# Gates of a mixture of experts: from sixteen spreading products to a DMA through DRAM, with the schedule around it rewritten

## The chip, the cores and the metric

The kernel runs on one core of one Trainium2 chip. The metric is the device time of one execution in microseconds. An engine is named as in the profile: PE is TensorE, DVE is VectorE, ACT is ScalarE, POOL is GpSimd, SP is SyncE.

## What is computed

One block over an input of 16 images of 56 x 56 tokens with 32 channels: windowed attention (windows of 7 x 7, shifted by 3, four heads of 8 channels, a bias table and a mask added after the softmax), a residual, and a mixture of experts with a residual. Cut to what matters:

```python
x = x + conv(layernorm(x))            # windowed attention, then out @ w_proj + b_proj
t = to_tokens(x)
probs = softmax(ln(t) @ router_w + router_b)      # 8 experts
top_p, top_i = top_k(probs, 2); top_p /= sum(top_p)
expert_out = einsum('bnd,edc->bnec', ln(t), expert_w) + expert_b
t = t + einsum('bnk,bnkc->bnc', top_p, take(expert_out, top_i))
```

## The kernel before

The work is cut into 16 units of 3136 tokens: two images, half of the columns. A tile of tokens has 112 partitions (image and row) with 28 tokens of 32 channels (896 elements). For products the channels of four tokens stand on 128 partitions (A = 4), with 784 columns.

The stages of a unit, with their names in the code and the lines of the profile:

- load (SP, L505, twelve DMAs into xin) and keep (SP, L512, one DMA xin to x_kept, two buffers; it waits until the residual of the unit two earlier, `back` 1, has read that buffer). The load of the next unit waits until keep has landed.
- norm1: a sum on DVE (L844), centring on POOL (L556), squares on ACT (L681), their sum on DVE (L850), then on POOL a scaling, an epsilon and a power of -1/2 (L567), and a multiplication (L571). norm2 is the same on the residual (L856, L579, L690, L862, L590, L594).
- xt (PE transposes L1111, ACT), qk (four products of 128x128 weights, L1119), place (POOL, q masked by head, L603) and kmask (ACT, k masked by head, L721), v (L1128), ob (L1143).
- attention in four groups. Of each: products for the maximum (PE L1161 into ps_win), the maximum and its split in two bf16 parts (DVE L866, L880, L882), their turn (PE L1169), a copy mr (ACT L766), the scores with the maximum taken off (PE L1184, L1190, into ps_win again), exponentials (ACT L776), products with v (PE L1205), a reciprocal and a product (DVE L889, L893) and the bias part added (POOL L611).
- ot (turned output), y (projection L1228, with b_proj added by a product of three bf16 parts, L1225), back (the residual on DVE, L907).
- x2t, router (PE L1251, tokens stationary), top2 (22 small steps on DVE and POOL: the two largest of eight logits, their shares, then the shares split in three bf16 parts), wt (turned to 96 x 784), mix (sixteen products L1273, each spreading one row group of shares over 128 partitions in ps_weight, each followed by a DVE product with the tokens, L979), the expert products (PE L1287 into ps_acc), final.
- replicate (SP, L522 and L525): the normalized tokens are copied so that each expert's 32 partitions hold them (x4). store (SP, L531).

Every engine runs the same generated list, `program`, and takes its own steps out of it, strictly in order. `macro_step` yields the four groups of one unit and, between their steps, the side tasks of `SIDE_TASKS`: of the unit after (xt, qk, v, ...), of the one after that (load, norm1), of the one before (y, norm2, router, top2) and of the one before that (mix, final, store). A place (g, p) of the table stands behind the scores (0), the maximum (1), the pv (2) and the shift (3) of group g. PE transposes and products of the side tasks share one PSUM bank, ps_shared, the mix has ps_weight, the expert sums ps_acc, the attention ps_win (four banks) and ps_pv.

## Time and profile before

| what | time |
|---|---|
| median of 3 runs | 838.19 us |
| lowest and highest | 836.32, 843.77 us |
| the profiled execution | 836.74 us |
| its span, first to last instruction | 834.9 us |
| mean granted clock of TensorE | 0.908 of full |
| busy: PE, DVE, ACT, POOL | 676.2, 547.7, 386.1, 486.1 us |

The span is what the rows below add up to; 1.8 us of the execution lie around it. In these rows a line with x16 is a group of sixteen instructions, the number before the engine is the start, the next the duration, and a bracket at the end is the idle time of that engine before it, with what ended it.

### The profile page before, as it was taken

The page shows a single profiled execution, that of the slowest core. Times are in us where ns is not written, and L with a number is a line of the kernel's source. Part 1 is how long each engine was busy: PE and PEld are TensorE (multiplying, and loading weights), DVE is VectorE, ACT ScalarE, POOL GpSimd, SP SyncE. Part 2 cuts the span into 40 slices and gives each one's busy share as a digit, 9 for nine tenths or more (in the row PEclk, how much of TensorE's full clock was granted, in tenths as well). Part 3 has the DMA queues.
Part 4 walks back from the last instruction along what each step waited for, and adds up shares of the span by engine and source line. Part 5 has one row for each costly group of instructions (what it writes and reads, how often), then busy time and mean ns, then how long its engine had stood idle before and what let it go on. Part 6 is the DMA issues. An engine that isn't in the chain of part 4 may idle for free.

```text
span 834.9 us, 29295 instructions
## 1 busy us (share of the span) xinstructions
PE 676.2 (81%) x12514; PEld 443.7 (53%) x12514; DVE 547.7 (66%) x999; ACT 386.1 (46%) x705; POOL 486.1 (58%) x539
## 2 busy tenths in 40 slices
PE   0787879888887879889797988888898988878666
PEld 0465555655556556546565554555656655645331
DVE  6242657768586767678676667857676767766443
ACT  1645464646364455626464463635355563622110
POOL 4616676575757666664757566574766666541520
PEclk9979989999999999988989889999999999997555
DMA  4100221413231131413231131323223230403040
GB/s 128 30 3 3 57 62 41 90 50 79 61 79 50 32 79 47 93 41 79 60 80 50 28 84 41 79 59 69 51 50 70 54 86 22 88 13 79 20 97 19
DMA packets 19008, 48.11 MB, mean 58 GB/s; under 512 B 9536, under 2 KB 9536, under 8 KB 17344
## 3 DMA queue, kind: packets, MB, share of 16 engines
q1 hardware_dynamic: 18448, 45.06, 23.3%
q8 instruction: 99, 1.62, 0.8%
q10 hardware_dynamic: 432, 1.19, 0.4%
q14 instruction: 29, 0.24, 0.1%
HBM read 7.69 MB, written 6.42 MB: 17 GB/s over the span
## 4 chain that ended last, share of the span: by engine, by line
PE 45%; DVE 32%; issue 11%; ACT 6%; POOL 4%; DMA 0%; SPq 0%; DVEq 0%; ACTq 0%; POOLq 0%
DVE mx L866 9%; PE ps_shared L1119 6%; PE ps_win L1190 6%; PE ps_acc L1287 5%; PE ps_pv L1205 5%; PE ps_shared L1143 4%; PE ps_weight L1273 4%; PE ps_win L1161 4%; PE ps_shared L1228 3%; DVE zt L979 3%; DVE x L979 3%; DVE x L907 2%; PE ps_win L1184 2%; DVE ms L880 2%; ACT ot L754 2%
## 5 line engine op out<-in xcount | busy, mean ns | idle before, releaser
L866 DVE TENSOR_REDUCE mx<-ps_win 128x32 f32<-128x1568 f32 x64 | 114.5, 1789 | 64.6 <-PE ps_win L1161 64.1
L979 DVE TENSOR_TENSOR zt<-ps_weight,x 128x392 f32<-128x392 f32 x118 | 66.1, 561 | 89.5 <-PE ps_weight L1273 89.0
L776 ACT ACTIVATE pt<-ps_win 128x784 f32<-128x784 f32 x128 | 98.4, 821 | 44.0 <-PE ps_win L1190 43.6
L1273 PE MATMUL ps_weight<-wt,const_bf_tile 96*128 96x392 bf16 x234 | 84.1, 359 | 41.1 <-DVE zt L979 20.7
L611 POOL TENSOR_TENSOR on<-on,obs 128x256 f32<-128x256 f32 x64 | 46.6, 729 | 120.0 <-DVE on L893 92.6
L1205 PEld LDWEIGHTS ps_pv<-vb,pt 128*49 128x49 f32 x4096 | 104.9, 129 | 15.3 <-issue 13.0
L1205 PE MATMUL ps_pv<-vb,pt 128*49 128x18 f32 x4096 | 109.7, 201 | 0.0
L979 DVE TENSOR_TENSOR x<-ps_weight,x 128x392 f32<-128x392 f32 x116 | 65.4, 564 | 38.3 <-PE ps_weight L1273 36.9
L766 ACT COPY mr<-ps_win 128x512 bf16<-128x512 bf16 x64 | 37.5, 587 | 95.8 <-PE ps_win L1169 95.8
L1190 PE MATMUL ps_win<-qbd,kp 32*49 32x196 f32 x2048 | 79.0, 370 | 0.0
L590 POOL TENSOR_TENSOR st<-st,minus_half 112x28 f32<-112x28 f32 x16 | 77.0, 4812 | 1.3
L567 POOL TENSOR_TENSOR st<-st,minus_half 112x28 f32<-112x28 f32 x16 | 76.9, 4809 | 1.3
L603 POOL TENSOR_SCALAR qbd<-qp,const_tile 128x392 f32<-128x392 f32 x128 | 76.6, 611 | 0.2 <-issue 0.2
L1273 PEld LDWEIGHTS ps_weight<-wt,const_bf_tile 96*128 96x128 bf16 x234 | 23.5, 100 | 87.7 <-DVE zt L979 41.4
L721 ACT ACTIVATE kbd<-kp,const_tile 128x392 f32<-128x392 f32 x128 | 69.3, 620 | 0.0
L1119 PE MATMUL ps_shared<-xt,folded_tile 128*128 128x392 f32 x124 | 66.3, 621 | 1.8 <-ACT xt L699 0.7
L1161 PE MATMUL ps_win<-kbd,qp 32*49 32x196 f32 x2048 | 59.0, 338 | 7.4 <-ACT pt L776 6.8
L699 ACT ACTIVATE xt<-ps_shared 128x448 f32<-128x448 f32 (+1 forms) x31 | 16.4, 528 | 85.5 <-PE ps_shared L1111 85.5
L1161 PEld LDWEIGHTS ps_win<-kbd,qp 32*49 32x49 f32 x2048 | 35.0, 120 | 34.1 <-ACT pt L776 25.0
L744 ACT COPY obs<-ps_shared 128x256 f32<-128x256 f32 x62 | 20.1, 375 | 55.8 <-PE ps_shared L1143 55.8
L1190 PEld LDWEIGHTS ps_win<-qbd,kp 32*49 32x49 f32 x2048 | 42.1, 131 | 4.2
L1169 PE MATMUL ps_win<-const_bf_tile,ms 128*128 128x128 bf16 x256 | 27.1, 232 | 20.4 <-DVE ms L882 20.1
(134 smaller groups left out, 1318.8 us busy)
## 6 DMA issues: line engine op xcount, KB each, us to landing
x<-x SPq DMA_DIRECT2D x48, 392.0 KB, 5.1
x_kept<-xin SPq DMA_DIRECT2D x16, 392.0 KB, 3.4
x<-x2t SPq DMA_DIRECT2D x64, 98.0 KB, 2.2
xin<-x SPq DMA_DIRECT2D x32, 150.0 KB
out<-xo SPq DMA_DIRECT2D x32, 150.0 KB
xin<-x SPq DMA_DIRECT2D x32, 18.0 KB
out<-xo SPq DMA_DIRECT2D x32, 18.0 KB
weight_tile<-weights ACTq DMA_DIRECT2D x1, 560.0 KB, 4.6
```

The costliest lines, as they stand in the source:

```text
L567: nc.gpsimd.tensor_tensor(st1[:, 4, :], st1[:, 3, :], minus_half[:, :], ALU.pow).then_inc(rstd1, 1)
L590: nc.gpsimd.tensor_tensor(st2[:, 4, :], st2[:, 3, :], minus_half[:, :], ALU.pow).then_inc(rstd2, 1)
L603: nc.gpsimd.tensor_scalar(qbd[i][:, :, h, :], qp[v.par][:, 8 * i:8 * i + 8, :], head_rows[:, h:h + 1], 1.0, ALU.mult, ALU.mult).then_inc(q ...
L721: ins = nc.scalar.activation(kbd[i][:, :, h, :], kp[v.par][:, 8 * i:8 * i + 8, :], ACT.Copy, scale=head_rows[:, h:h + 1])
L776: nc.scalar.activation(pt[g % 2][:, k, :, :, :].rearrange("p a h n -> p a (h n)"), ps_win[:, :, HN * k:HN * k + HN], ACT.Exp).then_inc(pro ...
L866: nc.vector.tensor_reduce(mx[g % 2].rearrange("n a x h -> n a (x h)"), ps_win[:, :, 0:8 * N].rearrange("n a (k m) -> n a k m", m=N), AX, A ...
L979: nc.vector.tensor_tensor(tokens if eh else zt[:, a, :], weight_bank(w, 1 + i)[:, 0:HALF], tokens, ALU.mult).then_inc(weight_drained, 1)
L1119: mm(pre_bank(v, 2 + i)[:, 0:HALF], (wk if i % 2 else wq)[:, :], xt[:, 8 * b:8 * b + 8, :, :].rearrange("p q k i -> p (q k i)"), start=Tru ...
L1161: ins = mm(ps_win[PAD * k:PAD * k + N, a, HN * x:HN * x + HN], qp[u.par][r, q, :], kbd[g // 2][r, q % 8, :, :].rearrange("p h n -> p (h n) ...
L1190: ins = mm(ps_win[PAD * k:PAD * k + N, a, HN * x:HN * x + HN], kp[u.par][r, q, :], qbd[g // 2][r, q % 8, :, :].rearrange("p h n -> p (h n) ...
L1205: ins = mm(ps_pv[PAD * x:PAD * x + N, c0:c0 + SLOT], pt[g % 2][:, x, a, h, :], vb[u.par][:, 2 * g + x, a, h, :], start=True, stop=True)
L1273: mm(weight_bank(w, 1 + i)[:, 0:HALF], weight_sel[:, eh, a, :], wt[:, HALF * half:HALF * half + HALF], start=True, stop=True).then_inc(wei ...
```

## The change

Eight edits, of which the first brings most of the new code.

1. The sixteen products that spread the shares are gone, and with them the three bf16 parts, wt and ps_weight. The shares (98 partitions, f32) are turned on PE, drained by ACT, written by SP to a DRAM tensor (four DMAs), and read back with a source stride of zero over the 32 partitions of an expert (eight DMAs into `gates`, four for experts 0 to 3, four for 4 to 7). The multiplication with the tokens is split between DVE and POOL (`mul`, half each), and the expert sums (`sum`) run over a left part of 448 and a right part of 336 columns.
2. ps_weight becomes a second bank of ps_shared; all side fills alternate between the two, and a fill waits for the drain two fills back.
3. The router keeps its weights stationary (`route`) and its result is turned (`logits`): the top 2 work on 98 partitions with 32 tokens.
4. q and k are each made by products on 64x64 quadrants (`project`), both halves together.
5. The root is found without a power: ACT takes a logarithm and an exponential (`norm_scale`), DVE makes one Newton step in three instructions (`norm_root`), POOL multiplies. The table of ACT is loaded once, ahead of everything, in both kernels.
6. b_proj is added by POOL to the kept input (`kept`), not by a product.
7. The second half of kmask goes from ACT to POOL.
8. The table of side tasks, the prologue and the tail are written anew.

The core of the diff:

```diff
 SIDE_TASKS = {
-    (0, 0): [("ot", 1), ("keep", 0), ("wt", 0), ("y", 0), ("mix", 0), ("back", 0), ("mix", 1), ("y", 1), ("back", 1), ("norm2_center", 0)],
...
-    (1, 0): [("qk", 0), ("load", 0), ("mix", 5)],
...
-    (2, 0): [("mix", 8), ("x2t", 0), ("norm1_center", 0), ("mix", 9)],
...
+    (0, 1): [("load", 0), ("y", 0)],
+    (0, 2): [("back", 0), ("share", 0), ("q", 0), ("y", 1)],
+    (0, 3): [("back", 1), ("gates", 0), ("norm2_center", 0)],
+    (1, 0): [("k", 0), ("norm1_center", 0)],
...
+            def gate_rows(w, _):
+
+                sp.wait_ge(shares_drained, upto("shares_drained", w))
...
+                for b in range(4):
+                    sp.dma_start(shares_kept[:, BLOCK * b:BLOCK * b + BLOCK],
+                                 shares[32 * b:32 * b + 32, :]).then_inc(shares_stored, 16)
+                sp.wait_ge(shares_stored, upto("shares_stored", w))
...
+                for eh in range(2):
+                    for e in range(4):
+                        rows = bass.AP(shares_kept.tensor, shares_kept.offset + (4 * eh + e) * COLS,
+                                       [[0, C], [E * COLS, A], [1, COLS]])
+                        sp.dma_start(gates[C * e:C * e + C, eh, :, :], rows).then_inc(gates_high if eh else gates_low, 16)
...
-                nc.gpsimd.tensor_tensor(st1[:, 4, :], st1[:, 3, :], minus_half[:, :], ALU.pow).then_inc(rstd1, 1)
...
+                nc.scalar.activation(st1[:, 1, :], st1[:, 2, :], ACT.Ln, bias=eps1[:, 0:1]).then_inc(log1, 1)
...
+                nc.scalar.activation(st1[:, 3, :], st1[:, 1, :], ACT.Exp, scale=-0.5, bias=guess_scale[:, 0:1]).then_inc(guess1, 1)
...
+            def mul(w, i):
+
+                eh, half = divmod(i, 2)
+                dve.wait_ge(x4_ready, upto("x4_ready", w))
+                if eh:
+                    dve.wait_ge(gates_high, upto("gates_high", w))
+                else:
+                    dve.wait_ge(gates_low, upto("gates_low", w))
+                gate = gates[:, eh, 0:2, columns(half)]
+                nc.vector.tensor_tensor(gate, gate, x4[w.par][:, 0:2, columns(half)], ALU.mult).then_inc(gated, 1)
...
+                for b in range(2):
+                    for r in range(2):
+                        rows, to = slice(64 * r, 64 * r + 64), 64 * (r ^ b)
+                        ins = mm(halves[b][to:to + 64, 0:HALF], w64[rows, rows],
+                                 xt[rows, 8 * b:8 * b + 8, :, :].rearrange("p q k i -> p (q k i)"), start=True, stop=True)
```

Three places of the new order. First VectorE, from the residual (back 0 and 1, writing x) over the sum of norm2 to the loaded input's sum (st<-xin), in one unit. Before:

```order
L907 TENSOR_TENSOR x_1<-ps_shared,x_kept 112x3x4x32
L856 TENSOR_REDUCE st<-x_1 112x28
L866 TENSOR_REDUCE mx<-ps_win 128x32
...
L866 TENSOR_REDUCE mx<-ps_win 128x32
...
L979 TENSOR_TENSOR zt<-ps_weight,x_0 128x392
L844 TENSOR_REDUCE st<-xin 112x28
L979 TENSOR_TENSOR zt<-ps_weight,x_0 128x392
L866 TENSOR_REDUCE mx<-ps_win 128x32
```

and in the changed kernel, where gates<-gates is the multiplication of a half of the low gates:

```order
L999 TENSOR_TENSOR x_0<-ps_shared,x_kept 112x3x4x32
L934 TENSOR_REDUCE st<-x_0 112x28
L908 TENSOR_REDUCE st<-xin 112x28
L958 TENSOR_REDUCE mx<-ps_win 128x32
L972 TENSOR_SCALAR ms<-mx 128x8x4
L974 SCALAR_TENSOR_TENSOR ms<-mx,ms 128x8x4
L981 RECIPROCAL rz<-ps_pv 128x32
L985 TENSOR_TENSOR on<-ps_pv,rz 128x16x2x8
L940 TENSOR_REDUCE st<-sq 112x28
...
L1061 TENSOR_TENSOR gates<-gates,x_1 128x2x448
L958 TENSOR_REDUCE mx<-ps_win 128x32
```

The input's sum has moved from behind two maxima after the residual to right behind the sum of norm2, and a wait for gates stands ahead of the third maximum.

Second SyncE's queue, from keep to the copies of the tokens. Before:

```order
L512 DMA x_kept<-xin 112x896
L505 DMA xin<-x 48x800
...
L505 DMA xin<-x 3x96
L522 DMA x_1<-x2t 32x784 x4
L525 DMA x_1<-x_1 32x3136 x3
```

and in the changed kernel:

```order
L495 DMA x_kept<-xin 112x896
L488 DMA xin<-x 48x800
...
L488 DMA xin<-x 3x96
L519 DMA shares_kept<-shares 32x196 x4
L528 DMA gates<-shares_kept 32x4x784 x8
L506 DMA x_0<-x2t 32x784 x4
```

The twelve transfers that were in the queue between keep and the copies are still there, and four writes and eight reads of the gates have come in behind them.

Third ScalarE, around the copy mr of group 2. Before:

```order
L776 ACTIVATE pt<-ps_win 128x784 x2
L710 ACTIVATE qp<-ps_shared 128x392
L714 COPY kp<-ps_shared 128x392
L766 COPY mr<-ps_win 128x512
L710 ACTIVATE qp<-ps_shared 128x392
```

and in the changed kernel, where st<-st,eps is the logarithm and st<-st,guess_scale the exponential:

```order
L803 ACTIVATE pt<-ps_win 128x784 x2
L740 COPY kp<-ps_shared 128x392 x2
L704 ACTIVATE sq<-xc 112x896
L760 COPY vb<-ps_shared 49x64x8 x2
L818 ACTIVATE st<-st,eps 112x28
L822 ACTIVATE st<-st,guess_scale 112x28
L793 COPY mr<-ps_win 128x512
```

The logarithm and the exponential, which take VectorE's sum of squares, stand ahead of mr.

## Rows read from the trace of the kernel before

**Rows 1.** Windows: length, busy PE, PEld, DVE, ACT, POOL, clock, DMA share, GB/s

```profile
0.00:39.30 39.30, 17.01 (x157) 10.11 (x157) 19.77 (x46) 14.34 (x26) 21.56 (x32) 0.96 0.29 84
...
120.60:685.50 564.90, 483.10 (x9386) 321.16 (x9385) 403.33 (x720) 287.65 (x529) 363.92 (x397) 0.95 0.27 62
...
640.80:685.50 44.70, 38.10 (x772) 25.66 (x770) 33.05 (x60) 23.89 (x45) 30.26 (x33) 1.00 0.28 65
...
775.40:834.90 59.50, 37.48 (x161) 16.04 (x161) 27.05 (x56) 5.73 (x10) 13.27 (x13) 0.53 0.21 46
```

**Rows 2.** Timeline of one group of the unit, all engines

```profile
656.36 1.79 DVE L866 TENSOR_REDUCE mx<-ps_win 128x32 f32<-128x1568 f32 x1 [1.14 <-PE ps_win L1161]
...
658.19 0.24 DVE L880 TENSOR_SCALAR ms<-mx 128x32 bf16<-128x32 f32 x1
...
659.07 0.35 DVE L889 RECIPROCAL rz<-ps_pv 128x32 f32<-128x32 f32 x1
...
659.25 0.59 ACT L766 COPY mr<-ps_win 128x512 bf16<-128x512 bf16 x1 [1.61 <-PE ps_win L1169]
...
659.45 0.42 DVE L893 TENSOR_TENSOR on<-ps_pv,rz 128x256 f32<-128x256 f32 x1
...
660.66 0.67 PE L1190 MATMUL ps_win<-qbd,kp 32*49 32x196 f32 x16
```

**Rows 3.** Lines of PE within that unit (busy us, mean ns | idle before)

```profile
L1205 PE MATMUL ps_pv<-vb,pt 128*49 128x18 f32 x256 | 6.6, 198 | 0.0
...
L1273 PE MATMUL ps_weight<-wt,const_bf_tile 96*128 96x392 bf16 x16 | 5.4, 337 | 3.2 <-DVE x L979 1.7 <-DVE zt L979 1.4
...
L1119 PE MATMUL ps_shared<-xt,folded_tile 128*128 128x392 f32 x8 | 3.6, 532 | 0.1
...
L1228 PE MATMUL ps_shared<-weight_tile,ot 128*112 128x128 f32 x14 | 1.9, 273 | 0.0
...
L1111 PE MATMUL ps_shared<-const_tile,xc 112*128 112x112 f32 x7 | 1.0, 263 | 0.5 <-POOL xc L571 0.5
```

**Rows 4.** Lines of DVE and POOL within that unit

```profile
L979 DVE TENSOR_TENSOR zt<-ps_weight,x 128x392 f32<-128x392 f32 x8 | 4.5, 560 | 5.9 <-PE ps_weight L1273 5.9
...
L567 POOL TENSOR_TENSOR st<-st,minus_half 112x28 f32<-112x28 f32 x1 | 4.8, 4807 | 0.1
```

**Rows 5.** Timeline of PE, from the last maximum to the next scores

```profile
676.17 0.91 PE L1161 MATMUL ps_win<-kbd,qp 32*49 32x196 f32 x32
...
684.41 0.67 PE L1190 MATMUL ps_win<-qbd,kp 32*49 32x196 f32 x16
```

**Rows 6.** Timeline of SP's queue in the prologue and that unit, and of DVE

```profile
13.62 4.27 SPq L505 DMA_DIRECT2D xin<-x  x12
...
19.04 0.53 SPq L512 DMA_DIRECT2D x_kept<-xin  x1
...
646.82 1.09 DVE L856 TENSOR_REDUCE st<-x 112x28 f32<-112x896 f32 x1
...
647.17 0.54 SPq L512 DMA_DIRECT2D x_kept<-xin  x1
...
650.59 4.28 SPq L505 DMA_DIRECT2D xin<-x  x12
...
665.19 2.44 SPq L522 DMA_DIRECT2D x<-x2t  x4
...
669.23 2.43 SPq L525 DMA_DIRECT2D x<-x  x3
```

**Rows 7.** Windows while constants are loaded and while x2t is copied

```profile
4.00:5.00 1.00, 0.00 (x0) 0.00 (x0) 0.89 (x3) 0.00 (x0) 0.00 (x0) 1.00 0.99 381
...
667.00:668.00 1.00, 0.91 (x10) 0.80 (x9) 0.99 (x3) 0.59 (x2) 0.53 (x1) 1.00 0.82 185
```

**Rows 8.** Timeline of POOL and DVE, one pass beside a small instruction

```profile
648.31 1.75 POOL L579 TENSOR_TENSOR xc<-x,st 112x896 f32<-112x896 f32 x1
...
649.64 0.51 DVE L880 TENSOR_SCALAR ms<-mx 128x32 bf16<-128x32 f32 x1
```

More of the change, by code:

```diff
@@ L20 @@
+import math
 from contextlib import ExitStack
@@ L166, in macro_step, with program @@
         yield from side((g, 3))
-def program(eng):
-    unit = [fixed(n) for n in range(UNITS)] + [None, None]
+def program():
+    unit = [None, None] + [Unit(n) for n in range(UNITS)] + [None, None]
     seen = []
@@ L543, in _ @@
                     replicate(unit, i)
+                elif step == "gates":
+                    gate_rows(unit, i)
                 elif step == "store":
@@ L805, in _ @@
             act.dma_start(const_bf16_tile[:, :], consts_bf16).then_inc(weights_loaded, 16)
-            for step, unit, i in program(act):
+            for step, unit, i in program():
                 if step == "norm1_square":
@@ L1043, in _ @@
             ones(vb[0])
-            for step, unit, i in program(dve):
+            for step, unit, i in program():
                 if step == "norm1_center":
@@ L1048, in _ @@
                     norm1_scale(unit, i)
+                elif step == "norm1_root":
+                    norm1_root(unit, i)
                 elif step == "norm2_center":
@@ L1298, in _ @@
             mm(ps_acc[:, 0:FOLDED], part["centre"], part["raw"], start=True, stop=True).then_inc(centred_weights, 1)
-            for step, unit, i in program(pe):
+            for step, unit, i in program():
                 if step == "xt":
```

669 lines of the change are left out of this document (353 added, 316 removed), and 16 rows, old and new, of tables (PROLOGUE, SIDE_TASKS, TAIL, per_unit).

## The prediction, made before the changed kernel was run

> **What bounds the kernel now.** I read the windows by stretch first, then the busy time by line within one undisturbed unit, then the timeline of that unit, and last the DMA queue of SyncE. The kernel is one loop over 16 units, and no stretch of it looks unlike the rest: from the scores of unit 2 to those of unit 14, twelve units take 564.9 us, 47.1 us each, with TensorE at 0.95 of its full clock; the undisturbed unit from 640.8 takes 44.7 us and keeps TensorE busy for 38.1 of them, VectorE for 33.1, GpSimd for 30.3, ScalarE for 23.9 [rows 1]. So TensorE is nearest to being the bound, but not alone: a unit holds four groups, and each group is a serial chain through one PSUM tile, ps_win. From the start of the maximum on VectorE to the start of ScalarE's copy mr it takes 2.9 us (maximum 1.8, two small instructions, and 0.5 for the turn on TensorE), the copy 0.6, and the scores end 1.5 us after it, of which I count 1.4 [rows 2]. Ahead of it come the exponentials and the products for the maximum. Whatever is queued ahead of one of these steps on its engine and waits, delays the unit.
>
> **What leaves TensorE.** The 16 products that spread the weights over partitions are 5.4 us of TensorE per unit and another 3.2 of waiting for VectorE [rows 3]. The projections, 3.6 us per unit, are cut into 64x64 quadrants; that they run side by side is what the products on 32-row tiles already do, so I take half, 1.8 us. Together TensorE falls by about 7 us per unit, from 38 to 31. VectorE loses 16 products of 0.56 us, 9.0 in all, and gets four multiplications of 896 or 672 elements, about 1.1 and 0.8 us by the 1.09 us of its reduction over 896 [rows 4, 6]. GpSimd loses two powers of 4.8 us and gets half of the k masks, the bias on the kept input and four multiplications of up to 1.7 us, which is what a pass over 896 elements takes it [rows 4, 8]. Every engine gets room. If nothing new waited, I work a unit out at 43 us below.
>
> **What is moved, and what is queued behind it.** Here the order decides. All times are from the end of a unit's first scores (time 0); the walk follows the program's order with the durations of the rows.
>
> Step 1, until back 1. The roots, three small VectorE instructions (0.2 each as an estimate, about half the 0.35 of the reciprocal in [rows 2]), and GpSimd's 1.7 [rows 8] now stand ahead of xt: 2.3. Then on TensorE xt 1.0, maximum 0.9, y 0 1.0, pv 1.6; on VectorE the reciprocal and product of pv 0.8 and back 0 0.6 (like a product of 392 elements); q 0.9, its drain 0.5 (mr's copy of 512 columns takes 0.59), y 1 0.9, back 1 0.6 [rows 2 to 5]. Sum: 11.1, say 11.
>
> Step 2, the load. keep copies xin into a buffer that back 1 of the unit two earlier reads last, so on SyncE it waits for back 1, as before; but the load now stands right behind it and the sum over the loaded input (norm1_center) stands two VectorE instructions after back 1, ahead of the next maximum. Before, the sum came more than a group later. From the rows: back 1 ends where the sum behind it starts, at 646.8, keep is issued at 647.17, the load may start at 650.59, so 3.8 us; and from the load's first issue at 13.62 to the instruction that waited for its landing 5.4 us [rows 6]. The input is there at 11 + 3.8 + 5.4 = 20.2. VectorE has 1.1 us of work in between (the sum of norm2), so it stands for about 8 us, and the maximum of group 2, whose products TensorE has ready at about 15, starts at 20.2 + 1.1 = 21.3 in place of 15. I find no cover: TensorE can do pv and v meanwhile and is then idle.
>
> Step 3, the second scores. The small instructions of the maximum end at 23.7. ScalarE's logarithm and exponential of norm2 now stand ahead of its copy mr and wait for VectorE's reciprocal and product (0.8) and the reduction over squares (1.1); with 0.5 for the two themselves (an estimate by VectorE's small ones of 0.24 and 0.35), mr starts at 26.1, ends at 26.7, and the scores end at 28.1. The same happens one group later with norm1. Each costs 2 us where the power on GpSimd had cost this path nothing.
>
> Step 4, the gates. SyncE ends the issue of the load at 11 + 3.8 + 4.3 = 19.1. Four small writes of the shares follow, and the reads wait for them: four copies out of x2t, equally many, let the next transfer start 4.0 us after the first issue [rows 6], so the reads start at 23.1. They are eight of 401 KB (32 partitions, 4 runs of 3136 bytes), 3.2 MB per unit. The trace of before has no such read. The nearest rows are the x2t copies, with the same run and the same 32 partitions: 185 GB/s at a share of 0.82, 226 GB/s full; the upper end is the load of the constants, 381 GB/s at 0.99 [rows 7]. I take 226, the nearer: 7.1 us for the low half and 14.2 for both, after 2.3 us of fixed time (4.0 less 0.4 MB at 226). Low lands at 32.5, high at 39.6. At 381 they land at 29.6 and 33.8. A source row that 32 partitions read at once could also be slower, for which no row gives a price; I bound it at half the rate, 39.6 and 53.8.
>
> Step 5, the third and fourth scores. VectorE's first multiplication waits for low ahead of the third maximum: 32.5 + 1.1 = 33.6, the maximum's small instructions end at 36.0, norm1's reduction, logarithm and exponential as in step 3 give 38.4, mr and scores 40.4. The third multiplication on GpSimd is done at 39.6 + 1.7 = 41.3; sum 1 on TensorE waits for it, ahead of the next unit's maximum: 42.2 (0.9, as one projection has it, since its four products use different columns of the array), maximum 43.1. From the end of this maximum to the end of the scores the unit before took 8.0 us (677.08 to 685.08, [rows 5]); one more sum of 0.9 stands in it now. The unit ends at 52.0.
>
> **The Trainium skill against this.** A small VectorE instruction took 0.51 us at 649.64 while GpSimd ran its 1.75 us pass, and 0.24 in the quiet group [rows 2, 8]. "SBUF — State Buffer", section "SBUF: two separate sides", says that a VectorE instruction with two SBUF inputs and a GpSimd instruction that reads SBUF exclude each other for the whole instruction. The multiplications on both engines are released by the same transfer, so by that rule the third maximum could come 1.7 us later than I have it; the trace agrees in kind. Likewise "DMA: Bandwidth & Descriptors", section "Latency and other measured facts", says that the receipt is the fixed part of a transfer and slowest from HBM, so the writes of the shares may cost more than my 4.0 us; no row here shows it.
>
> **The sum.** Up to the first scores of unit 0: 39.3 [rows 1], less one power of 4.8 for about 1.3 of its successor, and some of the bias preparation: 34.8. The next two units took 81.3 (39.3 to 120.6); the first has no stall (SyncE is ahead), the second has the load but no gates: 38 + 46 = 84. Twelve units of 52: 624. The last two took 89.9; without loads, with gates on a free queue, 85. The tail took 59.5 [rows 1]: the last unit's roots save 4, but the way from the shares to the products is a write and 3.2 MB of reads (20 us) where 16 products took some 14 us, net 61. Sum: 34.8 + 84 + 624 + 85 + 61 = 889, against a span of 834.9; with the 1.8 us that lie around the span (836.7 executed, within the 836.3 to 843.8 of the runs, whose median is 838.2) 891.
>
> **Rivals.** (a) Faster: the waits don't bind. Mechanism: if the load lands within 4 us of back 1, and the gates before the third maximum, the unit is the walk without them: scores at 21.9, maximum at 24.3, 31.1, and 43 at the end; all in all 776 us. It decides at 47.5 us a unit, above which the kernel is slower. For it: TensorE gives up 7 us, and VectorE waits 5.9 us in a unit for those products alone. Against it: 3.8 and 5.4 us are in the trace and the order leaves no room. (b) Reads at 381 GB/s: the third maximum is then held only by step 3, the unit takes 49.6, the kernel 862. (c) The clock and the port: TensorE idles 5 us twice per unit. In the tail, with gaps of that kind, its clock was 0.53 [rows 1]. At 1.2 GHz turn and scores cost 1.7 us more twice, and shared reads as much: 55.5 a unit, 933. (d) The reads from one row are slow, half the rate: 66 a unit, with the tail and the last two units 1090. (e) All within 1%: a unit of 47 to 48, part of each wait.
>
> **How the numbers follow.** My forecast holds 0.50, (a) 0.14, (b) 0.13, (c) 0.13, (d) 0.06, (e) 0.04. The time is that of the forecast, 891, whose own range is 870 to 915. The range of 830 to 950 leaves out (a) and (d). Runs of this kernel spread by about 1%, which is what can be told. Faster: (a), 0.14; within 1%: 0.04; slower: the rest, 0.82.
>
> **What would show it.** In the profile of the changed kernel the VectorE reduction over xin (L908) should be idle for about 7 to 8 us before each of 13 units, put down to the DMA into xin; the first multiplication (L1061) should wait 4 to 6 us on the DMA into gates; mr (L793) should wait longer in groups 2 and 3 than in 1; TensorE should be busy for about 31 us of a 52 us unit with a clock below 0.9. A loaded input within 5 us of back 1, or gates that land before the third maximum's products, would make the prediction wrong on the fast side; gates reads far under 226 GB/s on the slow side.

## The result and the profile after

| what | time |
|---|---|
| changed kernel, median of 4 runs | 1011.36 us (1011.17 to 1012.46) |
| before, median of 4 runs | 837.26 us (834.82 to 843.77) |
| ratio | 1.207, 95% interval 1.200 to 1.214 |
| span of the profiled execution | 1009.6 us, TensorE's granted clock 0.757 |

Ratios and their intervals, here and below, leave out executions more than 1.5% slower than the fastest of the same kernel; medians do not.

Slower, as forecast, but by 174 us where 53 were forecast, and outside the range. The windows of the changed kernel, with the columns of [rows 1]: one unit from back 1 to back 1, twelve units, all behind them, and inside the unit the stretch from the turn of group 2's maximum to that of group 3's.

```profile
437.60:496.10 58.50, 41.39 (x751) 26.68 (x751) 36.09 (x54) 23.83 (x47) 32.52 (x32) 0.76 0.48 107
143.90:846.80 702.90, 488.77 (x9156) 319.74 (x9140) 424.31 (x637) 282.38 (x552) 389.42 (x384) 0.77 0.48 107
846.80:1009.60 162.80, 84.68 (x1345) 50.28 (x1345) 79.91 (x120) 37.32 (x74) 71.16 (x56) 0.66 0.58 125
449.00:466.00 17.00, 11.04 (x171) 6.84 (x175) 12.94 (x17) 7.32 (x15) 13.61 (x11) 0.54 0.93 198
```

A unit takes 58.6 us (702.9 / 12) where it took 47.1, and no engine is busy for more than 42 of them: the kernel waits. TensorE is busy for 41.4 us of the unit, where I had forecast about 31. Between 449 and 466 the clock is 0.54, so nearly at its lower level of 1.2 GHz, after TensorE had stood for 5 us.

The groups by line over the whole execution, which answer to [rows 3, 4]:

```profile
L654 POOL TENSOR_TENSOR gates<-gates,x 128x896 f32<-128x896 f32 x64 | 147.5, 2313 | 30.1 <-DMA gates<-shares_kept 30.1
L1061 DVE TENSOR_TENSOR gates<-gates,x 128x896 f32<-128x896 f32 x64 | 75.5, 1186 | 76.6 <-DMA gates<-shares_kept 76.0
L1350 PE MATMUL ps_acc<-gates,folded_tile 128*32 128x336 f32 (+1 forms) x512 | 73.4, 656 | 85.3 <-POOL gates L654 48.1 <-DVE gates L1061 35.2 <-ACT ym L853 1.9
L1034 DVE SCALAR_TENSOR_TENSOR logits<-pick,logits 98x256 f32<-98x256 f32 x16 | 24.8, 1549 | 0.6
L908 DVE TENSOR_REDUCE st<-xin 112x28 f32<-112x896 f32 x16 | 17.4, 1086 | 108.6 <-DMA xin<-x 108.6
```

Both forecast waits are there: VectorE stands 108.6 us for the input and 76.0 for the gates. What was not forecast: GpSimd's multiplication takes 2.3 us (a mean over its two sizes), and one small step of the top 2 takes 1.5 us, nearly as long as a maximum (1.8). Now the timelines of the unit whose first scores end at 427.0 (start, duration). SyncE's queue, which answers to [rows 6]:

```profile
437.67 0.54 SPq L495 DMA_DIRECT2D x_kept<-xin  x1
441.08 4.92 SPq L488 DMA_DIRECT2D xin<-x  x12
446.44 1.70 SPq L519 DMA_DIRECT2D shares_kept<-shares  x4
449.27 3.90 SPq L528 DMA_DIRECT2D gates<-shares_kept  x8
```

VectorE:

```profile
447.28 1.09 DVE L908 TENSOR_REDUCE st<-xin 112x28 f32<-112x896 f32 x1 [8.56 <-DMA xin<-x]
448.28 1.78 DVE L958 TENSOR_REDUCE mx<-ps_win 128x32 f32<-128x1568 f32 x1
...
459.07 1.09 DVE L1061 TENSOR_TENSOR gates<-gates,x 128x896 f32<-128x896 f32 x1 [2.17 <-DMA gates<-shares_kept]
460.08 1.78 DVE L958 TENSOR_REDUCE mx<-ps_win 128x32 f32<-128x1568 f32 x1
...
464.62 0.85 DVE L1061 TENSOR_TENSOR gates<-gates,x 128x672 f32<-128x672 f32 x1
...
467.12 1.44 DVE L1061 TENSOR_TENSOR gates<-gates,x 128x896 f32<-128x896 f32 x1 [1.66 <-DMA gates<-shares_kept]
...
477.77 1.71 DVE L1034 SCALAR_TENSOR_TENSOR logits<-pick,logits 98x256 f32<-98x256 f32 x1
479.52 0.86 DVE L1061 TENSOR_TENSOR gates<-gates,x 128x672 f32<-128x672 f32 x1
```

GpSimd beside it:

```profile
459.11 2.99 POOL L654 TENSOR_TENSOR gates<-gates,x 128x896 f32<-128x896 f32 x1 [0.43 <-DMA gates<-shares_kept]
463.79 2.27 POOL L603 TENSOR_TENSOR on<-on,obs 128x256 f32<-128x256 f32 x1 [1.68 <-DVE on L985]
466.01 4.50 POOL L654 TENSOR_TENSOR gates<-gates,x 128x672 f32<-128x672 f32 x2
...
477.42 1.79 POOL L654 TENSOR_TENSOR gates<-gates,x 128x672 f32<-128x672 f32 x1
```

And TensorE, which answers to [rows 5]:

```profile
450.99 0.61 PE L1236 MATMUL ps_win<-const_bf_tile,ms 128*128 128x128 bf16 x4 [5.06 <-DVE ms L974]
...
459.99 2.86 PE L1273 MATMUL ps_pv<-vb,pt 128*49 128x18 f32 x64
...
476.06 0.40 PE L1236 MATMUL ps_win<-const_bf_tile,ms 128*128 128x128 bf16 x4 [0.40 <-DVE ms L974]
476.38 1.11 PE L1207 MATMUL ps_shared<-vb,bt 128*64 128x256 f32 x12
480.43 0.77 PE L1350 MATMUL ps_acc<-gates,folded_tile 128*32 128x336 f32 x8 [2.93 <-DVE gates L1061]
481.13 1.11 PE L1284 MATMUL ps_shared<-const_tile,on 128*128 128x128 f32 x4
482.04 1.70 PE L1300 MATMUL ps_shared<-const_tile,ym 128*112 128x128 f32 x7
483.67 0.38 PE L1251 MATMUL ps_win<-mr,const_bf_tile 32*49 32x196 bf16 x8
```

The last five rows are the place where the walk was most off: between the turn of the next unit's first maximum (476.1) and its scores (483.7) stand a sum that waits 2.93 us for the fourth multiplication, a turn and final. The multiplication is late because L1034 ahead of it ran 1.71 us beside GpSimd's multiplication of 1.79.

### The profile page after: what moved, and what is told of

Same layout as the page of the kernel before. It is cut to its first block, busy times and chain, and to the rows that moved or that the text cites. A ratio compares the mean times of both kernels' runs of the same rounds, so it can differ in the third digit from the quotient of the medians.

```text
span 1009.6 us, 28917 instructions
## 1 busy us (share of the span) xinstructions
PE 669.9 (66%) x12210; PEld 435.6 (43%) x12210; DVE 571.1 (57%) x878; ACT 378.3 (37%) x737; POOL 516.5 (51%) x522
## 3 DMA queue, kind: packets, MB, share of 16 engines
q8 instruction: 97, 1.59, 0.7%
## 4 chain that ended last, share of the span: by engine, by line
PE 32%; DVE 22%; DMA 13%; issue 12%; SPq 7%; POOL 7%; ACT 7%; ACTq 0%; DVEq 0%; POOLq 0%
PE ps_pv L1273 7%; DMA gates<-shares_kept 6%; SPq L488 5%; DMA x_kept<-xin 4%; DVE mx L958 4%; PE ps_acc L1350 4%; PE ps_win L1228 4%; PE ps_win L1257 4%; PE ps_shared L1293 3%; POOL gates L654 3%; DVE logits L1034 2%; ACT pt L803 2%; DMA xin<-x 2%; DVE x L999 2%; PE ps_shared L1182 2%
## 5 line engine op out<-in xcount | busy, mean ns | idle before, releaser
L654 POOL TENSOR_TENSOR gates<-gates,x 128x896 f32<-128x896 f32 x64 | 147.5, 2313 | 30.1 <-DMA gates<-shares_kept 30.1
L603 POOL TENSOR_TENSOR on<-on,obs 128x256 f32<-128x256 f32 x64 | 67.0, 1047 | 151.6 <-DVE on L985 116.6
L1273 PE MATMUL ps_pv<-vb,pt 128*49 128x18 f32 x4096 | 130.7, 214 | 3.3 <-issue 3.3
L1350 PE MATMUL ps_acc<-gates,folded_tile 128*32 128x336 f32 (+1 forms) x512 | 73.4, 656 | 85.3 <-POOL gates L654 48.1
L1061 DVE TENSOR_TENSOR gates<-gates,x 128x896 f32<-128x896 f32 x64 | 75.5, 1186 | 76.6 <-DMA gates<-shares_kept 76.0
L1257 PE MATMUL ps_win<-qbd,kp 32*49 32x196 f32 x2048 | 98.9, 456 | 0.2 <-issue 0.2
L1251 PE MATMUL ps_win<-mr,const_bf_tile 32*49 32x196 bf16 x1024 | 45.2, 328 | 52.2 <-ACT mr L793 52.2
L908 DVE TENSOR_REDUCE st<-xin 112x28 f32<-112x896 f32 x16 | 17.4, 1086 | 108.6 <-DMA xin<-x 108.6
L569 POOL TENSOR_TENSOR xc<-xc,st 112x896 f32<-112x896 f32 x16 | 27.1, 1697 | 80.7 <-DVE st L927 80.7
L1236 PEld LDWEIGHTS ps_win<-const_bf_tile,ms 128*128 128x128 bf16 x256 | 21.4, 122 | 103.3 <-DVE ms L974 80.1
L760 ACT COPY vb<-ps_shared 49x512 f32<-49x512 f32 x64 | 37.9, 592 | 38.7 <-PE ps_shared L1192 38.3
```

Of the source, the lines that this page charges most:

```text
L603: nc.gpsimd.tensor_tensor(o, o, obs[u.par][:, g, :, :, :, :].rearrange("p k a h d -> p (k a h d)"), ALU.add).then_inc(o_ready, 1)
L654: nc.gpsimd.tensor_tensor(gate, gate, x4[w.par][:, 2:4, columns(half)], ALU.mult).then_inc(gated_pool, 1)
L1061: nc.vector.tensor_tensor(gate, gate, x4[w.par][:, 0:2, columns(half)], ALU.mult).then_inc(gated, 1)
L1236: ins = nc.tensor.transpose(ps_win[:, 0, 0:256].bitcast(BF16)[:, 128 * h:128 * h + 128], ms[g % 2][:, h, :], identb[:, :])
L1251: mm(ps_win[PAD * k:PAD * k + N, a, HN * x:HN * x + HN], shift_sel[r, x, :], mr[g % 2][r, :, k, 0:N], start=True, stop=False)
L1257: ins = mm(ps_win[PAD * k:PAD * k + N, a, HN * x:HN * x + HN], kp[u.par][r, q, :], qbd[g // 2][r, q % 8, :, :].rearrange("p h n -> p (h n) ...
```

## The experiments

All but the last two (c_best3, c_best4) are single runs, each with one run of the kernel before beside it (834.1 to 839.3 us). A single run tells some 8 us, the 1% by which runs of one kernel differ. The ten runs of c_best4 go from 826.7 to 846.0, so there a single run tells less.

**The two waits (943.0, 999.9, 918.9 us).** e_kept3 gives the kept input a third buffer:

```diff
-                if v.has_before(2):
-                    sp.wait_ge(token_drained, upto("token_drained", v.before(2), 1))
-                sp.dma_start(x_kept[v.par]...
+                if v.has_before(3):
+                    sp.wait_ge(token_drained, upto("token_drained", v.before(3), 1))
+                sp.dma_start(x_kept[v.number % 3]...
```

> The changed kernel with three buffers for the kept input in place of two: keep no longer waits for back 1 of the unit two earlier, so load and the gates behind it on SyncE start some 10 us earlier in a unit; nothing is left out. Theory of the waits (two waits in a row, both put there by keep): L908 idle falls from 108.6 us to under 20, the low gates land at about 22 us after the first scores in place of 32.1, L1061 idle falls to under 20, a unit takes 46 to 50 us in place of 58.6, the kernel 870 to 910. Rival, the reads themselves: 14 us of reads at 205 GB/s stay on the path, L1061 stays at 60 us or more, the kernel above 960. Rival, clock and port: only the waits' own share goes, VectorE and GpSimd stretch each other as before, L654 stays at 2.3 us, 930 to 960.

e_no_gates takes the gates' transfers away, so that the spreading of the shares is left out:

```diff
-                elif step == "gates":
-                    gate_rows(unit, i)
...
+            nc.gpsimd.memset(gates[:, :, :, :], 0.125).then_inc(gates_set, 1)
```

> The changed kernel without the writes of the shares and the reads into the gates tile (it holds a constant from the start, so the shares don't reach the output: the spreading of the shares is left out); all multiplications stay. Theory of the waits: the wait for the load stays as it is (L908 idle about 108 us), the wait for the gates goes; the third scores come 6 us earlier, a unit takes 50 to 53 us, the kernel 920 to 950. Rival, the reads are the whole cost: 840 or below. Rival, clock and port: the multiplications still run side by side, so under 40 us are gained, above 970.

e_both has both edits.

> Both edits together: three buffers for the kept input, and no writes of the shares and no reads into the gates tile (the spreading of the shares is left out). Theory of the waits: neither wait is left, a unit takes 42 to 45 us, the kernel 780 to 830, and about what the kernel with three buffers alone gives plus at most 60. If the two savings add up exactly, the waits are independent; the theory has them one behind the other, so that each alone gives 60 to 130 us and both together 180 to 230. Rival, clock and port: still above 880, with L654 at 2.3 us and the clock below 0.85.

Measured: 68.3 us, 11.4 us and 92.4 us below the changed kernel. Without the gates alone the saving is 11.4, but 24.1 once the load's wait is gone: a part of the gates' wait stands behind the load's, as the theory had it. But the two together give only 12.7 us more than their sum, where the theory had 180 to 230 in all, and in all three runs the time fell where the rival, clock and port, had it: 943.0 (930 to 960), 999.9 (above 970), 918.9 (above 880, with the clock at 0.779 and below the 0.85 named). In e_both VectorE is idle 14.4 us for the input and nothing for gates, and the kernel is still 84 us slower than the one before. The groups of e_both:

```profile
L635 POOL TENSOR_TENSOR gates<-gates,x 128x896 f32<-128x896 f32 x64 | 123.4, 1941 | 0.1
L1330 PE MATMUL ps_acc<-gates,folded_tile 128*32 128x336 f32 (+1 forms) x512 | 71.8, 643 | 67.4 <-DVE gates L1041 49.4
L888 DVE TENSOR_REDUCE st<-xin 112x28 f32<-112x896 f32 x16 | 17.3, 1084 | 14.5 <-DMA xin<-x 14.4
```

TensorE waits 49.4 us for VectorE's multiplications though no gate has to arrive. From keep to keep (181.56 to 763.92, eleven units) a unit takes 52.9 us, where I had worked out 43 for a unit without these waits. That is 9.9 us more. The two waits themselves cost less than forecast, 5.7 us a unit (58.6 less 52.9) in place of 9.

**e_center_late (1001.7 us).** The sum over the input three steps later:

```diff
-    (1, 0): [("k", 0), ("norm1_center", 0)],
+    (1, 0): [("k", 0)],
-    (1, 3): [("kept", 0), ("norm2_root", 0)],
+    (1, 3): [("kept", 0), ("norm2_root", 0), ("norm1_center", 0)],
```

> The changed kernel with the sum over the loaded input (norm1_center) three steps later: behind norm2_root, after the shift of the second group instead of ahead of the maximum. Nothing is left out. Theory of the waits: the load's wait of 8 us per unit goes from ahead of the third maximum (L908 idle under 20 us in all), but the gates land as late as before (they wait for back 1 through keep), so VectorE waits for them instead: L1061 idle rises from 76.6 to 130 us or more and the kernel stays within 25 us of 1011. Rival, each wait costs by itself: 13 times 6 us less, 930 to 940.

Its groups:

```profile
L1061 DVE TENSOR_TENSOR gates<-gates,x 128x896 f32<-128x896 f32 x64 | 73.4, 1154 | 158.0 <-DMA gates<-shares_kept 157.5
```

The input's wait is gone, the gates' wait has doubled from 76.0, and 9.7 us are gained, little more than one run can tell, of the 78 (13 times 6) that the other view gives.

**One piece of the order at a time, on e_kept3 (943.0 us).** k_scale (932.5), k_q_late (912.7), k_sum3 (957.1), k_mul_dve (926.2); plus marks a step of the unit before:

```diff
 k_scale
-    (1, 2): [("v", 0), ("place", 0), ("norm2_scale", 0)],
+    (1, 2): [("v", 0), ("place", 0)],
+    (1, 3): [("norm2_scale", 0), ("kept", 0), ("norm2_root", 0)],
...
 k_q_late
-    (0, 2): [("back", 0), ("share", 0), ("q", 0), ("y", 1)],
+    (0, 2): [("back", 0), ("share", 0)],
+    (0, 3): [("y", 1), ("back", 1), ("gates", 0), ("norm2_center", 0)],
+    (1, 0): [("q", 0), ("norm1_center", 0)],
+    (1, 1): [("k", 0), ("norm2_square", 0)],
...
 k_sum3
+    (0, 0): [("sum+", 3), ("mix_drain+", 1), ("norm1_root", 0), ("final+", 0), ("final+", 1), ("store+", 0), ...
...
 k_mul_dve
-                gate = gates[:, eh, 0:2, columns(half)]
+                gate = gates[:, eh, :, columns(half)]
```

> Base is the changed kernel with three buffers for the kept input (943.0 us, a unit 54.3 us). Here also both norm_scale steps stand behind the shift of their group, so ScalarE copies mr before it takes logarithm and exponential. Nothing is left out. Theory of the order (what is queued ahead of the copy mr, of the scores and of the maximum costs its whole wait): TensorE's wait for mr in the group of norm2 falls from 2.55 to 0.7 us, that of norm1 from some 1 us, 1.9 to 2.5 us per unit, the kernel 905 to 925. Rival, the clock and the port set the time whatever the order: within 10 us of 943.

> Base as above (943.0 us). Here the products of q stand behind the scores of the next group, those of k one place later, and y 1 behind the shift, where q and y 1 stood between the products with v and the shift, each waiting for a drain of the shared bank. Nothing is left out. Theory of the order: the shift of the second group goes out when its maximum is split, at 454.9 in place of 459.5 in the unit read; y 1 then still waits for back 0 until about 456.4, so the scores end 3 to 4 us earlier, and the kernel takes 885 to 905. Rival, clock and port: within 10 us of 943.

> Base as above (943.0 us). Here the last expert sum, its drain, final and store stand behind the first scores of the next unit in place of ahead of them. Nothing is left out. Theory of the order: in the unit read mr is ready at about 494.7 but the scores start at 501.6, behind a sum that waits 2.7 us for the fourth multiplication, ot and final; the stretch from the fourth to the next first scores falls from 17.6 to 11 to 13 us, of which the next group gives back about 1 us for sum and final ahead of xt; the kernel takes 870 to 900. Rival, clock and port: within 10 us of 943.

> Base as above (943.0 us). Here VectorE makes the whole multiplication of gates and tokens (1792 and 1344 elements) and GpSimd none, so the two no longer run this on SBUF at the same time. Nothing is left out. Theory of the port (the two engines hold each other up on these multiplications): an uncontended VectorE does 1792 elements in 2.0 to 2.2 us and 1344 in 1.5 to 1.7, less than the 3.0 to 3.4 that both took side by side; GpSimd's addition to on (L603) falls from a mean of 1.11 us to about 0.75 and the logits step L1034 from 1.55 to under 1; the kernel takes 900 to 925. Rival, no port effect: VectorE gets 57 us more work ahead of the maxima and the kernel takes 960 or more.

k_scale gave 10.5, below the 18 to 38 expected and little more than one run can tell: TensorE's wait for mr fell from 54.9 to 33.3 us in all, but half of that went into other waits; the one for the gates stayed at 69.9. k_q_late gave 30.4, short of the 38 to 58 expected. k_sum3 missed in sign: the first scores do start sooner, but final waits for a drain that stands behind the exponentials on ScalarE, and holds the next maximum. TensorE in k_sum3, from the first scores' end:

```profile
452.46 0.77 PE L1351 MATMUL ps_acc<-gates,folded_tile 128*32 128x336 f32 x8 [0.74 <-DVE gates L1062]
453.17 0.65 PE L1301 MATMUL ps_shared<-const_tile,ym 128*112 128x128 f32 x4
456.44 0.86 PE L1301 MATMUL ps_shared<-const_tile,ym 128*112 128x128 f32 x3 [2.62 <-ACT ym L854]
457.09 1.06 PE L1285 MATMUL ps_shared<-const_tile,on 128*128 128x128 f32 x4
457.95 1.63 PE L1170 MATMUL ps_shared<-const_tile,xc 112*128 112x112 f32 x7
459.51 1.58 PE L1229 MATMUL ps_win<-kbd,qp 32*49 32x196 f32 x32
```

I had let the next group give back 1 us; 7.8 us pass here from the scores' end (451.7) to the maximum's products, where e_kept3 has 3.1. k_mul_dve gave 16.9, just short of the 18 to 43 expected. Its groups:

```profile
L1058 DVE TENSOR_TENSOR gates<-gates,x 128x1792 f32<-128x1792 f32 x32 | 70.0, 2186 | 52.5 <-DMA gates<-shares_kept 52.2
L1031 DVE SCALAR_TENSOR_TENSOR logits<-pick,logits 98x256 f32<-98x256 f32 x16 | 6.8, 425 | 0.6
```

The logits step falls from 1.55 to 0.43 us. VectorE does the whole of a left part in 2.19 us, while GpSimd took 2.54 us for its half of it in e_kept3: sharing the work between them bought nothing. (GpSimd's addition L603 did not fall, 1.40 in place of 1.11 us; it meets VectorE's multiplication still.)

**The clock: a_fill (1007.4 us).** Idle products ahead of waits. They start in the bank of the expert sums and so change these sums:

```diff
+                for _ in range(n):
+                    mm(ps_acc[:, 448:512], identb[:, :], identb[:, 0:64], start=True, stop=True, skip_group_check=True)
```

> The changed kernel (1011.4 us) with idle work on TensorE: 36 small bf16 products into unused columns of ps_acc ahead of the turn of the third and fourth group's maximum, where it waits 5.1 us in the unit read, and 24 ahead of the second and fourth expert sum, where it waits 1.1 and 2.9 us. Nothing is left out. Theory of the clock (the clock is low because TensorE stands, and what runs after a wait runs at half): the granted clock rises from 0.757 to 0.85 or more, products with v after the waits take 1.6 us in place of 2.9, and a unit loses 2 to 4 us, the kernel 960 to 990. Theory of the waits: TensorE isn't the bound where it idles, the clock gives back at most what stands on the chain after the waits, 990 to 1011. Rival, the filling delays the chain: 1015 or more.

The clock rose to 0.784, not to 0.85, and the time fell by 4 us, less than one run can tell. TensorE in the unit read:

```profile
441.25 1.22 PE L1234 MATMUL ps_acc<-const_bf_tile 128*128 128x64 bf16 x36
446.38 0.61 PE L1241 MATMUL ps_win<-const_bf_tile,ms 128*128 128x128 bf16 x4 [3.90 <-DVE ms L974]
...
455.37 2.86 PE L1278 MATMUL ps_pv<-vb,pt 128*49 128x18 f32 x64
...
460.57 1.88 PE L1234 MATMUL ps_acc<-const_bf_tile 128*128 128x64 bf16 x36
462.29 0.39 PE L1241 MATMUL ps_win<-const_bf_tile,ms 128*128 128x128 bf16 x4
```

The filling was too short for the first gap: 3.9 us of idleness were left and the products with v still took 2.86 us. Behind the second filling the turn takes 0.39 in place of 0.61. So this run neither prices the clock nor bounds it; what full speed would give there was not tried. What the traces show is its size in busy time: the four kinds of product of the attention's groups (for the maximum, taking it off, the scores, with v; L1161, L1184, L1190, L1205 before and L1208, L1231, L1237, L1253 in e_both) are the same in both kernels and keep TensorE busy for 16.7 us in the unit before from 640.4 to 685.1 and for 22.0 in the unit of e_both from 495.1 to 549.1. How much of these 5.3 us stands on the chain is open.

**Together, and on the changed kernel itself.** c_all (897.5) has kept3, k_scale, k_q_late and k_mul_dve; a_mul_dve (998.6) only the last of these on the changed kernel, a_order (955.0) the last three.

> The four edits that gave something, together: three buffers for the kept input, both norm_scale steps behind the shift, q behind the scores with y 1 behind the shift, and the whole multiplication on VectorE. Nothing is left out. On the 943.0 us of the first alone the others gave 10.5, 30.4 and 16.9. If they are independent: 885. If they stand one behind the other (the gates come at their own time whatever the rest does, so VectorE waits longer for them): above 900, with L1061 idle over 90 us in place of 71. If they open each other: below 870.

> The changed kernel (1011.4 us) with the whole multiplication on VectorE and nothing else changed. Theory of the port: 15 to 30 us less (981 to 996), by the logits step (L1034, 1.5 us, falls to 0.43) and by sum 1, which waits for GpSimd 2 us less per unit. Rival, the waits hide it: within 5 us of 1011.

> The changed kernel with two buffers for the kept input as it is, and three of the four edits: both norm_scale steps behind the shift, q behind the scores with y 1 behind the shift, the whole multiplication on VectorE. Nothing is left out. On top of three buffers the same three edits took 45.6 us off. Theory of the waits in a row: y 1 and so back 1 come 1 us later or earlier at most, keep, load and gates still hang on back 1, so the three edits give less here than there: 975 to 995. If they are independent of the waits: 966.

c_all is 12 us above the 885 of independent savings and 2.5 below the 900 of the other theory: the three pieces give 45.6 together on three buffers and 57.8 as a sum of single runs. Moving the multiplication is worth 12.8 us in the changed kernel, somewhat less than the 15 to 30 expected. The three pieces give 45.6 with three buffers and 56.4 without, more even than the 45.4 of the independent case; the waits do not hide them, against the theory, which had 16 to 36. And three buffers give 57.5 beside them, 68.3 alone. So the order and the waits are nearly independent causes.

**SyncE's queue: c_gates (962.1) and c_store (870.3).** On c_all, the load behind the gates, or the store behind them:

```diff
 c_gates
-    (0, 1): [("load", 0), ("y", 0)],
+    (0, 1): [("y", 0)],
+    (1, 0): [("load", 0), ("q", 0)],
...
+    (1, 3): [("norm2_scale", 0), ("kept", 0), ("norm2_root", 0), ("norm1_center", 0)],
...
 c_store
-    (3, 3): [..., ("final", 1), ("store", 0)],
+    (0, 3): [("y", 1), ("back", 1), ("gates", 0), ("store+", 0), ("norm2_center", 0)],
```

> The same as the kernel with the four edits together, and on SyncE the shares are written and the gates read ahead of the next load (load one group later, the sum over the loaded input behind norm2_root). Nothing is left out. Theory of the waits: the reads start 4 to 5 us earlier, so VectorE waits 4 us less per unit for the gates; the load gets 14 us of reads ahead of it and lands some 25 us after keep, ahead of where it is now needed or up to 3 us late: 25 to 50 us below the kernel without this edit. Rival, the load simply takes the place of the gates (L908 idle over 60 us): the same within 10 us.

> The kernel with the four edits together (897.5 us, a unit 50.0 us), and the store of a unit's result stands behind the next gates on SyncE in place of ahead of keep, load and gates. Nothing is left out. Theory of the queue (the twelve issues of the store, 4.9 us, hold keep, load and gates): keep is issued some 5 us earlier, VectorE's wait for the gates (L1058 idle, 75 us) falls below 35, the unit to 46 to 48, the kernel to 850 to 875. Rival, the reads take as long as before and the shares aren't ready sooner, so the gates land when they did: within 8 us of 897.5.

c_gates is 65 us slower than c_all. Its SyncE queue and VectorE:

```profile
470.85 4.00 SPq L527 DMA_DIRECT2D gates<-shares_kept  x8
474.94 4.33 SPq L488 DMA_DIRECT2D xin<-x  x12
```

```profile
491.01 1.08 DVE L905 TENSOR_REDUCE st<-xin 112x28 f32<-112x896 f32 x1 [9.79 <-DMA xin<-x]
```

The load, 5.4 us when alone [rows 6], is there 16 us after its first issue, with 3.2 MB ahead of it whose issue began 4 us earlier. That is 26 us after keep, as expected (25), but VectorE stands 9.8 us for it: I had priced its landing against keep and not against where it is needed. c_store went as expected: the wait for the gates (L1058) falls from 74.8 to 25.4 us, the kernel by 27 us. The twelve issues of a store that nobody waits for had held the input and the gates.

**The order alone: c_best1 (848.6), c_best2 (855.5), c_best3 (856.3), c_best4 (837.4).** On c_store, more side tasks moved, so that no wait stands between a turn and its scores. The last has, with a third residual buffer:

```diff
+    (2, 0): [("final+", 0), ("kmask", 0), ("norm1_square", 0), ("mul", 0), ("final+", 1), ("store+", 0)],
...
+    (2, 3): [("x2t", 1), ("norm1_scale", 0), ("route", 0), ("replicate", 0), ("mul", 2), ("mul", 3)],
+    (3, 0): [("v", 1), ("logits", 0), ("kmask", 1)],
+    (3, 1): [("place", 1), ("sum", 0), ("sum", 1), ("mix_drain", 0), ("top2", 0)],
+    (3, 2): [("sum", 2), ("sum", 3), ("mix_drain", 1), ("top2", 1)],
+    (3, 3): [("ob", 0), ("ob", 1), ("top2", 2), ("top2_exp", 0), ("ot", 0)],
```

> The kernel with the store behind the gates (870.3 us, a unit 47.2 us) with more of the side tasks moved and nothing else: the fourth multiplication right behind the third, the expert sums one to two places later so that none stands ahead of a maximum or a turn whose input is ready, the second x2t behind the turn, v 0 behind the turn. Nothing is left out. Theory of the order: the scores after the fourth group wait 3 to 4 us less (mr was ready 6.4 us before them in the unit read), the third and fourth group lose 1 to 2 us more: a unit 42 to 45, the kernel 820 to 845. Rival, something else holds it (reads, clock): within 10 us of 870.

> As the last, and further: final of a unit behind the first scores of the next, xt between the turn and the scores of the next group, y 1 and back 1 behind these scores, the first three side steps of the second half of the top 2 behind the maximum, both x2t and all sums behind the turns. Nothing is left out. Theory of the order: nothing that waits stands between a turn and its scores or ahead of a maximum; VectorE (35 us a unit) and the gates' way (13 us to the issue of the reads, 9.4 to the low half, 16.5 to both) are next: a unit 40 to 43, the kernel 795 to 830. Rival: the shares come 3 us later than in the last and the gates hold VectorE again (L1058 idle over 50 us), 835 or more.

> The 848.6 us kernel with a third buffer for the residual, so that final may run while TensorE waits for the exponentials of the third group; the first step of the top 2 behind the next unit's first maximum; v 1 in the same wait as final, the first ob behind the fourth scores. Nothing is left out. Theory of the order: 1.8 us (the maximum ahead of the top 2) and 2 to 2.7 us (final) per unit, of which the longer TensorE queue of the third group gives back about 1: 13 times 3, the kernel 800 to 820. Rival, TensorE at half clock is the bound in the third group and takes what the fourth gives: 840 to 855.

> As the last, but v 1 stays behind the fourth scores and both ob stand behind the turn of the next unit's first maximum, 1.3 us of which the copy mr doesn't cover. Nothing is left out. Theory of the order: 805 to 830, within 10 us of the last. Rival as before: 840 to 855.

c_best1 gained 21.7 of the 25 to 50 expected; c_best2 and c_best3 fell short of theirs by 25 us and more, into the range of their rivals, and c_best4 (805 to 830 expected) by 7. Between c_best1, c_best2 and c_best3 the difference is no more than single runs scatter. c_best4 against the kernel before: the medians are 837.4 (10 runs) and 838.4 us (13), the ratio 0.991 (0.986 to 0.996). So it is level with the kernel before, and not shown to be faster; it is 17% faster than the changed kernel with the same operations, but for where the multiplication runs and for the third buffers. Why c_best3 (median of 4 runs) loses 19 us to c_best4 by v 1 and ob alone stays open.

## Why the prediction was right or wrong

**Direction, steps 1, 2 and 4: right, the direction in part by luck.** The forecast had the kernel slower because of the two waits, and 776 us, so faster, without them. Without them it takes 918.9 us (e_both), still 84 more than before: the sign would have come out the same had both waits been wrong. The steps themselves hold. Back 1 ends 10.6 us after the first scores (11 predicted), the input is summed at 20.3 (20.2) after a wait of 8.56 us (8), thirteen times, the writes of the shares hold the reads back by 2.8 us (446.44 to 449.27; 4.0), the low gates are used at 32.1 (32.5) and the high ones at 40.1 (39.6), so the rate taken from the x2t copies (226 GB/s) nearly holds: 198 GB/s at a share of 0.93 in the window from 449 to 466. The x2t copies were the right row, and the load of the constants, rival (b), was not.

**Step 3: right in kind.** The scores of group 2, the second of the walk, end at 28.9 (28.1). But k_scale shows that taking the logarithm from ahead of mr gives 10.5 us in all and not 2 times 2 us per unit.

**Step 5: failed.** "GpSimd is done at 39.6 + 1.7 = 41.3" took the time of a pass alone; with the one ahead of it in the queue it took 4.50 (the row at 466.01), and it was done at 43.5. "From the end of this maximum to the end of the scores the unit before took 8.0 us ...; one more sum of 0.9 stands in it now": from the end of the maximum's products to the end of the scores it was 12.8 us and not 8.9, because the sum has to wait for a multiplication that itself stands behind a stretched step of the top 2 (the rows of TensorE above), and final behind it. I added the duration of a new instruction and not its wait. The unit ended at 58.3 in place of 52.0. By place: up to back 1 of the third unit 143.9 us against 129.8, twelve units 702.9 against 624, the rest 162.8 against 135.2. That is 120.6 us, 79 of them in the units. For the first and last part no run was made, but the trace shows a piece of the last: for the last unit I had 20 us from the shares to their products, and from the copy of the shares (972.1) to the end of the last multiplication (998.8) it takes 26.7, with the halves again side by side on VectorE and GpSimd, and TensorE waiting for GpSimd:

```profile
989.24 1.72 PE L1350 MATMUL ps_acc<-gates,folded_tile 128*32 128x448 f32 x8 [15.70 <-POOL gates L654]
```

**The 43 us for a unit without waits: wrong, and the larger error.** It stood under rival (a) and did not enter the sum, but it was my picture of the kernel: "Every engine gets room". e_both measures it at 52.9, so 9.9 us a unit more, while the miss of the forecast is 6.6 a unit: the waits, priced 3.3 us a unit too high, covered a part of this error. I had added busy times and one walk. What fills the difference is shown in pieces, each on another base, so they can't be added: q and y 1 ahead of the shift (30.4 us on e_kept3), the multiplication shared with GpSimd (16.9 on e_kept3), and the sums and final ahead of the scores (21.7 with others in c_best1). The store ahead of keep (27.2 on c_all) acts through the wait for the gates, which e_both doesn't have, and so is no part of it. TensorE's lower clock, by which the attention's products alone are busy 5.3 us longer in such a unit, is the rival that no run here settles. I looked at three moves and the change has some thirty.

**Rival (c), clock and port, was nearer** than the forecast, at 933, and I gave it 0.13; it is still 78 us short, as far as rival (d) at 1090 is above, whose slow reads the 198 GB/s rule out. A port's part is shown: 12.8 us on the changed kernel for the multiplication alone. The multiplication on GpSimd starts at 459.11, VectorE's ends at 460.16, and GpSimd's ends 1.94 us after that, at 462.10; L1034 ends 0.27 us after GpSimd's at 479.21. So of two such instructions one ends only behind the other. By the rule ("SBUF — State Buffer", section "SBUF: two separate sides", in the Trainium skill: an exclusive lock for the whole instruction) the trace agrees. On who waits it does not: there the one that starts first has the lock, but GpSimd's addition L603, recorded as starting at 463.79, 0.83 us ahead of VectorE's multiplication (464.62), takes 2.27 us in place of its 0.73, and VectorE's takes 0.85, no longer than at 479.52. It is so in eleven more units, in one of them with 3.27 us. The row that I gave for the rule in the prediction, L880 at 649.64, is an instruction with one input and so no case of the rule as I told it. I had weighed it for one place and at 1.7 us, and not for the small steps of the top 2, which have two SBUF inputs as well. The clock's part is open; that c_best4 is level with the kernel before at granted clocks of 0.80 to 0.84, against 0.88 to 0.91, shows that a low clock alone need not make it slow.

## What to carry to other kernels

A transfer in an in-order queue is as late as the last thing ahead of it: look at what nobody waits for (a store) and at what is large (3.2 MB) before counting the transfer. When a table of side tasks is rewritten, walk the whole unit and give every product its wait, not its duration; the walk of the old kernel does not carry over. Measure a unit with all forecast waits taken out before trusting what is left: here it was 52.9 us and not 43. Splitting an elementwise pass over two SBUF operands between VectorE and GpSimd gained nothing here and stretched the small instructions beside it.

## What was not expected of the hardware

In c_gates, c_store and the c_best kernels TensorE stops in the middle of a group of scores, with no wait on another engine. c_best1, TensorE and the window:

```profile
462.63 0.49 PE L1254 MATMUL ps_win<-qbd,kp 32*49 32x196 f32 x3
466.63 0.74 PE L1254 MATMUL ps_win<-qbd,kp 32*49 32x196 f32 x13 [3.52 <-issue]
```

```profile
462.70:466.60 3.90, 0.42 (x18) 0.05 (x2) 2.45 (x1) 1.35 (x4) 3.90 (x5) 1.00 1.03 208
```

In c_best1 it comes in the same group's scores in four units (2.9 to 4.4 us each), while the reads of the gates fill the DMA engines. The traces hold more on this than the views of engines: 16 KB packets of the queue that the profile calls instruction (q8, 97 of them in c_best1, 1.59 MB, 7.7 us apart at the median). Here one runs from 463.73 to 465.12, and TensorE goes on 1.5 us behind its end. Over all runs there are 48 stops of more than 1.5 us between two products of the same line that no engine ends, and in all 48 TensorE goes on 1.2 to 1.7 us after the end of such a packet. So it waits for its instructions, as far as times alone can tell; no run varied it. Stops of over 2.9 us stand only in runs with reads of the gates.

One of VectorE's smallest instructions, a product of 28 elements per partition, lasts 2.5 us beside the stop (0.19 alone), but that is another thing:

```profile
464.15 2.51 DVE L945 TENSOR_TENSOR st<-st 112x28 f32<-112x28 f32 x1 [1.80 <-ACT st L819]
464.55 2.06 POOL L641 TENSOR_TENSOR x_kept<-x_kept,weight_tile 112x896 f32<-112x896 f32 x1
```

It is that long in 14 units of c_best1, ten more than have the stop, and each time it ends 0.04 to 0.05 us after GpSimd's addition of b_proj (edit 6), another pair with two SBUF inputs each. The changed kernel has the same at L953 in the unit read (2.57 us, ending 0.04 us after L642). What moving this addition away from the root would give was not tried.
